# Graph layer on one Trainium2 core: eight buffer slots in the second edge phase, edge attributes transposed two tiles at a time, and the first edge product as two matmuls with zero-padded weights

## The reference, cut to what matters

```python
ef = relu(edge_attr @ We1 + be1) @ We2 + be2          # edge_attr: 106250 x 64, We1: 64 x 128, We2: 128 x 128
ef = ef * sigmoid(edge_weight[:, None] @ Wt + bt)
combined = concatenate([x[row], ef], axis=1)          # row = source node of the edge
msg = relu(combined @ Wn1 + bn1) @ Wn2 + bn2
out = segment_sum(msg, col, 6250) + x                 # col = destination node
x = layernorm(x + out)
```

## Time and profile before

| | |
|---|---|
| median of 3 runs | 2353.68 us (2346.05 to 2355.03) |
| the profiled execution | 2350.46 us, of which its span is 2348.7 us |
| mean granted PE clock | 0.887 of full |
| PE busy | 2036.1 us |
| DVE busy | 1396.6 us |
| ACT busy | 662.6 us |
| POOL busy | 1612.5 us |

### The profile page before, as it was taken

How to read it: one execution, slowest core, us unless ns; L and a number is a source line. 1 busy time by engine, 2 the same in 40 slices (tenths; PEclk the granted TensorE clock), 3 DMA queues, 4 the chain that set the end, 5 groups by cost and what they waited for, 6 DMA issues and landing times.

```text
span 2348.7 us, 47789 instructions
## 1 busy us (share of the span) xinstructions
PE 2036.1 (87%) x12602; PEld 1378.4 (59%) x12673; DVE 1396.6 (59%) x3735; ACT 662.6 (28%) x1413; POOL 1612.5 (69%) x1692
## 2 busy tenths in 40 slices
PE   6488888898888888888689989889889898898987
PEld 5265666666666666666555555555555555555554
DVE  5455666666666666666445566665666556665555
ACT  4111111111111111111143333433334333343332
POOL 4577777777777777777077776666667666676663
PEclk9698999999999999999699889888898888988887
DMA  7523333333333333332255454444444444544442
GB/s 193 139 83 83 87 89 86 92 91 91 92 92 85 88 92 92 91 92 78 66 153 130 123 129 123 119 124 113 120 123 125 117 111 120 123 125 117 118 111 57
DMA packets 260322, 251.50 MB, mean 107 GB/s; under 512 B 144303, under 2 KB 196144, under 8 KB 260270
## 3 DMA queue, kind: packets, MB, share of 16 engines
q1 hardware_dynamic: 205598, 140.29, 21.4%
q0 software_dynamic: 53648, 109.59, 19.4%
q10 hardware_dynamic: 1024, 0.98, 0.2%
HBM read 232.72 MB, written 13.22 MB: 105 GB/s over the span
## 4 chain that ended last, share of the span: by engine, by line
PE 62%; issue 12%; DVE 12%; DVEq 4%; POOL 4%; ACT 2%; DMA 1%; SPq 0%; ACTq 0%; POOLq 0%
PE ps L1619 9%; PE ps L1776 7%; PE ps L1604 7%; PE ps L1769 7%; PE ps L1786 7%; PE ps L1782 6%; PE ps L1611 6%; PE ps L1654 5%; PE ps L1793 3%; POOL T L688 3%; PE ps L1658 3%; DVEq L1201 2%; DVE G L1420 1%; DVE R L1264 1%; ACT G L901 1%
## 5 line engine op out<-in xcount | busy, mean ns | idle before, releaser
L688 POOL DMA_INDIRECT T<-y_rows,idx x832 | 791.0, 951 | 409.0 <-issue 239.5
L655 POOL DMA_INDIRECT G<-hi_rows,idx x832 | 810.8, 975 | 284.6 <-issue 269.1
L1769 PE MATMUL ps<-G 128*128 128x64 f32 x1664 | 243.9, 296 | 111.5 <-ACT G L901 111.3
L1604 PE MATMUL ps<-ident,G 128*128 128x128 f32 x832 | 202.6, 331 | 127.6 <-DVE XM L1268 49.5
L901 ACT ACTIVATE G<-G 128x512 f32<-128x512 f32 x208 | 131.0, 630 | 616.2 <-DVE G L1420 616.2
L1769 PEld LDWEIGHTS ps<-G 128*128 128x128 f32 x1664 | 228.8, 213 | 129.2 <-ACT G L901 125.9
L1776 PE MATMUL ps<-wN,G 128*128 128x128 f32 x1664 | 278.0, 320 | 0.0
L826 ACT ACTIVATE V<-ps 128x512 f32<-128x512 f32 x208 | 124.2, 597 | 523.1 <-PE ps L1611 522.5
L1194 DVE TENSOR_TENSOR V<-ps,V 128x512 f32<-128x512 f32 x208 | 142.4, 685 | 211.6 <-ACT V L826 210.8
L1782 PE MATMUL ps<-msg,wE 128*128 128x512 f32 x416 | 254.8, 700 | 0.0
L1619 PE MATMUL ps<-V,AwP 128*32 128x128 f32 x1940 | 247.7, 297 | 6.8 <-DVE V L1194 6.8
(11 more groups left out here) (178 smaller groups left out, 2365.7 us busy)
## 6 DMA issues: line engine op xcount, KB each, us to landing
T<-in_edge_weight SPq DMA_DIRECT2D x207, 256.0 KB, 3.5
Dbc<-block_destinations SPq DMA_DIRECT2D x69, 384.0 KB, 3.6
T<-in_edge_attr SPq DMA_DIRECT2D x207, 128.0 KB, 2.2
G<-hi_rows,idx POOLq DMA_INDIRECT x832, 2.9
T<-y_rows,idx POOLq DMA_INDIRECT x832
link<-scan_destinations SPq DMA_DIRECT2D x70, 56.4 KB
hi_rows<-T SPq DMA_DIRECT2D x12, 256.0 KB, 2.8
out<-T SPq DMA_DIRECT2D x46, 64.0 KB
```

The costliest lines, as they stand in the source:

```text
L655: pool.indirect_dma_start(out=G[:, s, t * C:(t + 1) * C], out_offset=None, in_=hi_d[:, :], in_offset=bass.IndirectOffsetOnAxis(ap=idx[:, s ...
L688: pool.indirect_dma_start(out=Yb[:, r, t * C:(t + 1) * C], out_offset=None, in_=y_d[:, :], in_offset=bass.IndirectOffsetOnAxis(ap=idx[:, r ...
L1604: pe.matmul(U[j][:, i * P:(i + 1) * P], G[:, s, t * C:(t + 1) * C], ident[:, :], is_transpose=True, start=(i == 0), stop=False, skip_group ...
L1769: ins = pe.matmul(ps[4][:, 0:W], hS[:, i * C:(i + 1) * C], ohB[:, i * W:(i + 1) * W], start=(i == 0), stop=(i == 3))
```

## The change

It does four things together. `RB` becomes 8, and a new constant `BQ = 4` keeps the rhythm of one finished block for each four quads, so that the loop body is now eight quads and two blocks long; index columns of a gather are kept in `idx[:, r % RG, 4 * (r // RG) ...]`. `LAG` becomes 8, so 45 blocks are finished in the loop and four behind it. The attributes are transposed two tiles at once: 128 edges by 2 x 64 attributes become 128 partitions by 128 edges, in two transposes instead of four. The first edge product then takes 128 rows: `wE1` holds `We1` twice, once above zeros and once below zeros, and each of the two matmuls takes 256 columns of `atS` and writes the tiles that its half of the rows belongs to. The attribute and weight loads of a slot now count on one semaphore.

```diff
-RB = 4
-LAG = 7
-LOOPED = NQ // RB + 1 - LAG
+RB = 8
+BQ = 4
+LAG = 8
+LOOPED = NQ // BQ + 1 - LAG
...
-        wE1 = sb("wE1", [EC, C])
+        wE1 = sb("wE1", [P, 2, C])
...
-        atS = msg[0:EC, 0:QE]
+        atS = msg[:, 0:2 * P]
...
+            def block_at(k, r):
+                return k * (RB // BQ) + (r // BQ - LAG)
+            first = LAG * BQ // RB
             for q in range(2 * RB):
                 edge(q, q % RB, q // RB, None)
-            with eng.Fori(2, LAG) as k:
+            with eng.Fori(2, first) as k:
                 for r in range(RB):
                     edge(k * RB + r, r, k, None)
-            with eng.Fori(LAG, NQ // RB - 1) as k:
+            with eng.Fori(first, NQ // RB - 1) as k:
                 for r in range(RB):
-                    edge(k * RB + r, r, k, k - LAG)
+                    edge(k * RB + r, r, k, block_at(k, r))
...
-            sp.wait_ge(s_fill, 6)
+            sp.wait_ge(s_fill, 7)
+            for i in range(2):
+                sp.dma_start(wE1[i * EC:(i + 1) * EC, i, :], We1).then_inc(s_we, 16)
...
                         dve.wait_ge(s_b["at"], t + 1)
                         need(dve, s_b["h1"], t)
-                        dve.tensor_copy(atS, ps[0][0:EC, :]).then_inc(s_b["atc"], 1)
+                        dve.tensor_copy(atS, ps[0][:, 0:2 * P]).then_inc(s_b["atc"], 1)
...
-                        pe.matmul(ps[1][:, :], wE1[:, :], atS, start=True, stop=True).then_inc(s_b["h1"], 1)
+                        out1 = ps[1][:, :].rearrange("p (t k e) -> p k t e", t=2, k=2)
+                        for i in range(2):
+                            ins = pe.matmul(out1[:, i], wE1[:, i, :], atS.rearrange("p (t e) -> p t e", t=2),
+                                            start=True, stop=True)
+                        ins.then_inc(s_b["h1"], 1)
                     if t is not None:
                         last = is_int(t) and t == NQ - 1
-                        pe.wait_ge(s_at[r], 16 * (k + 1) + 16 * last)
+                        pe.wait_ge(s_at[r], 32 * (k + 1) + 16 * last)
                         need(pe, s_b["atc"], t)
                         passed(pe, "pe")
-                        for i in range(4):
-                            ins = pe.transpose(ps[0][0:EC, i * P:(i + 1) * P], atB[:, r, i * EC:(i + 1) * EC],
+                        for i in range(2):
+                            ins = pe.transpose(ps[0][:, i * P:(i + 1) * P], atB[:, r, 2 * i * EC:2 * (i + 1) * EC],
                                                ident[:, :])
```

More of the change, by code:

```diff
@@ L195, in build @@
         xE, tE, yE = (V[:, i, :].rearrange("p (b c) -> p b c", b=MN) for i in range(3))
-        xF, aF, yF = xs[0][:, 0, :], xs[0][:, 1, :], yS[0][:, 0, :]
         rest = NB - LOOPED
+        xF, aF, yF = (T4[:, i * C:(i + 1) * C] for i in range(3))
+        xr, yr = (T4[:, (3 + i * rest) * C:(3 + (i + 1) * rest) * C] for i in range(2))
+        yrB = yr.rearrange("p (b c) -> p b c", b=rest)
         accD = acc[0:DC, 1, :]
@@ L264, in build @@
         s_gy = [sem(f"y_gathered_{i}") for i in range(RB)]
-        s_at = [sem(f"attributes_loaded_{i}") for i in range(RB)]
-        s_ew = [sem(f"edge_weights_loaded_{i}") for i in range(RB)]
+        s_at = [sem(f"edges_loaded_{i}") for i in range(RB)]
         s_b = {n: sem("edge_" + n) for n in ("at", "atc", "h1", "r1", "ef", "tw", "efs", "z", "zs", "h", "oh",
@@ L285, in build @@
                "back": s_g[3][1], "loaded": s_g[3][2], "t": s_ext}
-        s_3 = {"table": s_ew[1], "turn": s_at[1], "idx": s_b["idx"], "rows": s_gy[0], "dc": s_at[2],
-               "dt": s_at[3], "same": s_b["oh"], "at": s_at[0], "ew": s_ew[0], "t": s_b["at"],
+        s_3 = {"table": s_at[5], "turn": s_at[1], "idx": s_b["idx"], "rows": s_gy[0], "dc": s_at[2],
+               "dt": s_at[3], "same": s_b["oh"], "at": s_at[0], "ew": s_at[4], "t": s_b["at"],
                "tc": s_b["atc"], "h1": s_b["h1"], "r1": s_b["r1"], "ef": s_b["ef"], "tw": s_b["tw"],
                "efs": s_b["efs"], "z": s_b["z"], "zs": s_b["zs"], "h": s_b["h"], "sum": s_b["agg"],
-               "new": s_b["acc"], "stored": s_gy[1], "back": s_ew[2], "loaded": s_ew[3], "bt": s_gy[2]}
+               "new": s_b["acc"], "stored": s_gy[1], "back": s_at[6], "loaded": s_at[7], "bt": s_gy[2]}
         s_n = {"x": s_mx[0], "copy": s_m["nm"], "zero": s_m["cl"], "t": s_m["gT"], "max": s_m["dmax"], "rd": s_m["rd"],
@@ L549, in store, with turn @@
                     sp.dma_start(out[bass.ds(m * P, P), :], yF).then_inc(s_out[0], 16)
+                def turn(k, stores):
+                    for r in range(RB):
+                        if stores and r % BQ == 0:
+                            store(k * (RB // BQ) + (r // BQ - LAG - 1))
+                        q = k * RB + RB + r
+                        load(q, r, is_int(q) and q == NQ - 1)
+                first = (LAG + 2) * BQ // RB
                 for q in range(RB):
                     load(q, q)
[L553 to L563, removed]
+                with sp.Fori(0, first - 1) as k:
+                    turn(k, False)
+                for r in range(RB):
+                    if r >= BQ:
+                        if r == BQ:
+                            store(0)
+                    load(first * RB + r, r)
+                with sp.Fori(first, NQ // RB - 2) as k:
+                    turn(k, True)
+                turn(NQ // RB - 2, True)
+                for m in range((NQ // RB - 1) * (RB // BQ) - LAG - 1, LOOPED):
                     store(m)
@@ L908, in edge @@
                         act.activation(r1S, ps[1][:, :], ACT.Relu, bias=cols[:, 1:2]).then_inc(s_b["r1"], 1)
-                    if r == 0 and m is not None and (not is_int(m) or m < LOOPED):
-                        act.wait_ge(s_b["acc"], (m + LAG - 1) * RB)
+                    if r % BQ == 0 and m is not None and (not is_int(m) or m < LOOPED):
+                        act.wait_ge(s_b["acc"], (m + (LAG - 1)) * BQ)
                         need(act, s_f["o"], m)
@@ L976, in _ @@
             settled(dve.tensor_scalar(first, iotaF[0:1, 0:LOOPED], float(P), float(P), ALU.mult, ALU.add))
-            settled(dve.tensor_tensor(ahead, first, baseR[0:1, (LAG - 1) * RB:(LAG - 1 + LOOPED) * RB:RB], ALU.is_gt))
+            settled(dve.tensor_tensor(ahead, first, baseR[0:1, (LAG - 1) * BQ:(LAG - 1 + LOOPED) * BQ:BQ], ALU.is_gt))
             settled(dve.tensor_reduce(late[:, 0:1], ahead, AX.X, ALU.add))
@@ L1505, in _ @@
             pe.wait_ge(s_w2, 16)
+            pe.wait_ge(s_we, 32)
             for i in range(1, 4):
@@ L1737, in _ @@
                     passed(pe, "pe")
-                    pe.matmul(ps[2][:, 0:P], wE1[:, :], atT, start=True, stop=True).then_inc(s_3["h1"], 1)
+                    pe.matmul(ps[2][:, 0:P], wE1[0:EC, 0, :], atT, start=True, stop=True).then_inc(s_3["h1"], 1)
                     pe.wait_ge(s_3["r1"], t + 1)
```

44 lines of the change are left out of this document (23 added, 21 removed).

## The result

The changed kernel takes 2244.48 us (median; 2240.49 to 2253.54), the kernel before 2349.86 us beside it: a ratio of 0.956 (95% interval 0.952 to 0.960). The rival "the gathers bind everywhere" gave 2250. The profiled execution took 2253.54 us, the longest of its four, with a span of 2251.8 us. Some executions of one kernel take over 1.5% longer than its fastest, at a lower clock; the ratios leave them out.

The account below looks back on a forecast made before the run. POOL's gathers bound the stage before finished blocks, then PE, DVE's chain and the clock. From 1336.5, 44 turns of 21.06 us end at 2263.1, 66.3 less with the tail, giving 2284.2, stated as 2285; range 2248 to 2320.

Parts of the forecast that it names:

- the gathers bind everywhere: Rival for the second phase: POOL's gathers, 20.0 us a turn, set the pace throughout; time 2250, chance 0.22.
- The sign that the prediction named for this: DVE's wait for the gathers seen all through the second phase would mean 2250 instead of the forecast.
- The turn before: Four quads per finished block in the kernel before: three free quads, line 1799, the r = 3 quad and clock; 22.54 us.
- Transposes, 0.24 saved: PE's attribute transposes, two instead of four per quad: 0.22 us instead of 0.46, 0.24 less.
- First edge product, 0.09 saved: PE's padded first product per quad takes 0.95 us instead of 1.06, taken as 0.09 less; bounds nothing to 0.2.
- Copy and branch: DVE's chain behind r = 3: shorter copy saves 0.27 us a turn, rarer loop branch 0.22 on average.
- I keep the clock's 2.93: PE's stretch at 1.2 GHz behind each block's stall stays, costing 2.93 us a turn as before.
- my 21.06: Forecast turn of four quads after the change: 3 x 3.93 + 0.22 + 6.12 + 2.93 = 21.06 us.
- The rival that the clock falls: PE's work shrinks while waits stay, so its low-clock stretch doubles: 2.93 us more a turn, 2413; chance 0.05.
- the case that it cites from the Trainium skill: Matmuls that wait for a transfer at every tile fall back to the low clock each time.
- Eight slots at nothing: POOL's slots alone give nothing, but let it work through the stall; if that cover failed, 3.2 us a turn.
- `LAG` and the first stage: Finishing starts four quads later: line 1799 at 1336.5, 44 turns instead of 45, one more block behind the loop, 0.8 us.

Follow-up runs that it names:

- the chain's shortening: Kernel before with the changed kernel's layout, shared semaphore and `LAG`, and two Newton steps instead of three in the second phase: 2291.45 us, ratio 0.976.
- The padding alone: Changed kernel with four slots, body of four, four old transposes, and the first product as one matmul over 128 rows, lower 64 zeros: 2260.77 us, 0.963.
- the gathers are eased: Changed kernel without the gather of each quad's fourth tile, three gathers instead of four: 2109.40 us, ratio 0.899.
- the stall filled: Four old transposes, 64-row product, four slots, body of four, plus four unread 256-column matmuls per block where PE stalls behind r = 3: 2254.26 us, 0.960.
- the filler elsewhere: Kernel before with four unread 256-column matmuls per block in the quad with r = 1, where PE does not stall: 2374.31 us, ratio 1.013.
- two pairs: Eight against four slots, body of eight: 2299.15 and 2302.11 us with four transposes and 64-row product; 2244.48 and 2248.69 us with the new product.
- the body of eight: Changed kernel with four slots, a body of eight quads, four old transposes and the 64-row product: 2302.11 us, ratio 0.980.
- Two banks with 64-row weights: Changed kernel with four slots, body of four, each half of the rows multiplied by its own 64 weight rows into two banks: 2263.39 us, 0.964.

## Why the forecast missed: two terms mis-sized, and the bound just below

The bound of the kernel before and the parts of the turn were right, and two of the terms were not; together they took the turn past the margin to the gathers, and with that the bound was another one than forecast. The sign that the prediction named for this came: DVE waits for the gathers all through the phase.

**The turn before** (22.53) and what bounds it: right. Three gathers instead of four left it at 22.36, and the chain's shortening passed through to the time.

**Transposes, 0.24 saved:** right. They take 0.22 from start to start instead of 0.46.

**First edge product, 0.09 saved: mis-sized.** It is 0.29: 0.20 in the product, 1.06 to 0.86, and 0.09 in the product ahead of it, 0.95 to 0.86. My row for a product that fills the array was itself one that stood before a 64-row load. The bounds had a gain of 0.2 and nothing beyond, so a free quad of 3.73 lay outside "3.81 to 4.1". The padding alone shows this term by itself: 4.26 to 3.95.

**Copy and branch:** right. 0.42 instead of 0.68, and gaps of 1.09 and 0.57 alternately. With three gathers the quad with r = 3, free of the bound, is 17.86 - 3 x 3.73 - 0.22 - 0.36 (4% at the low level) = 6.09; forecast 6.12.

**"I keep the clock's 2.93": the step that failed.** It is 1.0 in the changed kernel, and 0.36 when the gathers are eased. I took the low stretch for a fixed sequel of a 2.2 us stall, as it is in the trace before. With the stall filled the low share falls from 26% to 2%; the filler elsewhere, the padding alone (clock 0.92) and the changed kernel (2.25 us stalls, clock 0.95) show that its amount changes although such stalls stay. Of the 3.2 us between my 21.06 and the 17.86 that the changed kernel would reach, 2.57 are the clock and 0.6 the quads. The right quad alone would have left the sum at 20.46, above the gathers; the right clock alone, with 1.0, gives 19.13, below them. The rival that the clock falls had the wrong sign. It also stretched the case that it cites from the Trainium skill to short waits; the last point of this text comes back to it.

**Eight slots at nothing:** right, by two pairs. The reason given for them (cover for POOL) was wrong: with four slots the turn is 20.18.

**The gathers' bound:** priced right, 2250, and given 0.22. The sum stood 1.06 us from it, and its largest term that could move with the edit was the clock's 2.93. The bound was the likelier outcome.

**`LAG` and the first stage:** line 1820 starts at 1344.6, 8.1 later than forecast, because the first gather starts 8.6 later than in the trace before (1186.2 against 1177.6). That part lies ahead of the second phase, and it scatters: in the variants with four gathers the first one starts between 1175.1 and 1188.9. The tail behind the last line 1820 is 24.3 us (2227.5 to 2251.8) instead of 18.5, where 0.8 more was forecast; the last gather now starts 3.1 us after that line. With 44 turns of 0.99 less, 8.1 later and 5.0 more of tail, the forecast's 2284.2 becomes 2253.7; measured 2253.5.

**What stays open** is why the low share differs at equal stalls. Counted as above, the old product with two Newton steps or with the body of eight has a low stretch behind every stall, even those of 1.4 us, and the changed kernel behind 18 of 23 stalls over 1.9 us. Two banks with 64-row weights have 0.83, the padding alone 0.92, with stalls near 2.48 in both; their free quads differ too (3.65 and 3.95), and the experiments do not part the form of the matmuls from the rhythm of the turn.

## What to carry to other kernels

Where a stage shows a granted clock well under full, treat that cost as a term that can move with any edit, and price the forecast with it gone as well as kept; then ask which engine's floor is reached first. Write down the floor of every other engine per turn (here 16 gathers of 1.25 us), and where the sum lands within a tenth of it, take the floor for the likelier case. Before reshaping data to fill TensorE's rows, try zeros in the missing rows, and unread matmuls in the stall: one edit of each kind gave 3.7% and 4.0% here, of the full change's 4.4%. These gains do not add up, because the same floor lies just below each of them.

## What the runs showed of the hardware

- A float32 product with 64 rows of weights between products with 128 rows cost 0.29 us: 0.20 in the product itself and 0.09 in the one before it. The same number of columns and passes with zero rows added is quicker. In the trace before, the 64-row load and the 128-row load behind the product start only with the operation that uses them; with 128 rows throughout they start 0.43 us ahead of it.
- Four instructions of 256 columns on alternate halves of the rows, into two banks, take 0.63 us; four on all 128 rows take 0.86. The Trainium skill, page "TensorEngine Tiling (Array Packing)", section "Theoretical Speedup", gives up to 2x where the contracted dimension is at most 64; here it is 0.86 / 0.63 = 1.4.
- Stalls of 2.1 to 2.5 us were followed by stretches at 1.2 GHz in some turns and not in others of the same execution, and the granted clock of the stage ran from 0.83 to 0.98 over kernels with such stalls. Stalls of 1.4 to 1.6 us had such stretches behind them too, with a clock of 0.90. With 32 us of idle pieces in 44 turns instead of 86 in 40, about 0.7 us a turn instead of 2.2, it was 0.99.
- The Trainium skill, page "TensorE: Matmul & The Clock Gate", section "HAM oscillation — how this bites in real kernels", says that a PE which waits at every tile falls back to the low clock. The filled stall agrees with it in direction (0.99 against 0.87 with the stall left open). In the gather-bound turn of the changed kernel, which waits more often, the clock is higher (0.95). But the waits in the Trainium skill's example are longer than the changed kernel's stalls (at most 2.6 us), and much longer than those of the old kernel's gather-bound stage (at most 1.0 us from 1200 to 1310), so neither stage is its case, and the prediction's remark that the trace does not agree with it does not hold.
